# Building a Mamba block's decay arguments by broadcast and a GpSimd clamp instead of small matmuls

## The reference

```
proj = hidden @ in_proj_w.T            # gate | x,B,C | dt
hBC  = silu(conv1d(hBC) )              # 4 taps, causal
dt   = softplus(dt + dt_bias);  A_dt = -exp(A_log) * dt      # 128 heads
A_cumsum = cumsum(A_dt within a chunk of 128 tokens)
Lmat = exp(segment_sum(A_dt))          # exp(cum[l] - cum[s]), l >= s, per head
M = (C @ B.T) * Lmat;  Y_diag = M @ (x * dt)
states = (B * exp(A_cumsum[-1] - A_cumsum)).T @ (x * dt)     # carried over the chunks
Y = Y_diag + (C @ states) * exp(A_cumsum) + D * x
y = rmsnorm(Y) * norm_w * silu(gate);  out = y @ out_proj_w.T
```

## Time and profile before

| | us |
|---|---|
| median of 3 runs | 2141.62 (2141.0 to 2141.75) |
| the profiled execution, its time | 2141.5 |
| its span, first to last instruction | 2139.8 |
| PE busy | 2102.7 |
| DVE busy | 1689.4 |
| ACT busy | 1401.8 |
| POOL busy | 881.4 |
| mean granted TensorE clock | 0.997 |

### The profile page before, as it was taken

How to read it: one execution, slowest core, us unless ns; L and a number is a source line. 1 busy time by engine, 2 the same in 40 slices (tenths; PEclk the granted TensorE clock), 3 DMA queues, 4 the chain that set the end, 5 groups by cost and what they waited for, 6 DMA issues and landing times.

```text
span 2139.8 us, 37480 instructions
## 1 busy us (share of the span) xinstructions
PE 2102.7 (98%) x13386; PEld 1732.0 (81%) x13386; DVE 1689.4 (79%) x2679; ACT 1401.8 (66%) x1918; POOL 881.4 (41%) x622
## 2 busy tenths in 40 slices
PE   7999998999999999999999999999999999999999
PEld 6788876888888888888888888888888888878887
DVE  7555468988888888888898889898888888876554
ACT  5322277878787777777787877787777778752221
POOL 1222134545454545444454544544544545422221
PEclk9999998999999999999999999999999999999999
DMA  5543224233333333232333333342333233255441
GB/s 201 177 146 138 61 94 125 90 109 103 100 112 101 105 96 108 95 122 91 100 112 101 101 98 114 105 122 96 100 101 112 90 104 109 97 186 177 135 147 40
DMA packets 128644, 241.89 MB, mean 113 GB/s; under 512 B 14048, under 2 KB 48608, under 8 KB 128224
## 3 DMA queue, kind: packets, MB, share of 16 engines
q1 hardware_dynamic: 128480, 239.73, 34.9%
HBM read 234.17 MB, written 5.51 MB: 112 GB/s over the span
## 4 chain that ended last, share of the span: by engine, by line
PE 90%; DVE 3%; issue 3%; ACT 2%; DMA 1%; POOL 1%; SPq 0%; DVEq 0%; POOLq 0%; ACTq 0%
PE ring L1013 35%; PE ring L1113 16%; PE bank L412 6%; PE bank_e L412 6%; PE yt L1094 6%; PE st L1078 4%; PE yt L1100 4%; PE xt L1065 3%; PE bank_e L424 3%; PE bank L424 3%; PE arg L1051 2%; PE xt L1026 1%; PE bank L654 1%; DMA w_raw<-w_in 0%; DVE xr L304 0%
## 5 line engine op out<-in xcount | busy, mean ns | idle before, releaser
L1013 PE MATMUL ring<-m_lnt,w_sb 128*128 128x512 f32 x3456 | 859.9, 399 | 1.2 <-DVE xc L1440 1.2
L1013 PEld LDWEIGHTS ring<-m_lnt,w_sb 128*128 128x128 f32 x3456 | 633.0, 189 | 127.1 <-DVE xc L1440 1.5
L1673 POOL TENSOR_TENSOR w_sb<-w_raw,w_sb 128x512 fp32r<-128x512 f32 x288 | 401.7, 1400 | 177.3 <-ACT w_sb L1246 177.0
L1688 POOL TENSOR_TENSOR ysq<-ysq,y 128x512 f32<-128x512 f32 x126 | 162.8, 1292 | 652.8 <-ACT y L1290 652.8
L1113 PE MATMUL ring<-wo,ygs 128*128 128x512 f32 x1536 | 369.4, 390 | 2.0 <-issue 2.0
L1113 PEld LDWEIGHTS ring<-wo,ygs 128*128 128x128 f32 x1536 | 287.3, 188 | 63.2 <-issue 2.6
L1440 DVE SCALAR_TENSOR_TENSOR xc<-ring,cw,xc 128x511 f32<-128x511 f32 (+2 forms) x384 | 286.0, 745 | 23.0 <-ACT xc L1258 13.9
L1258 ACT ACTIVATE xc<-ring,cb,cw 128x512 f32<-128x512 f32 x128 | 99.2, 775 | 215.4 <-PE ring L1013 215.4
L1678 POOL TENSOR_TENSOR wo<-wo_raw,wo 128x512 fp32r<-128x512 f32 x128 | 214.0, 1672 | 0.0
L1246 ACT ACTIVATE w_sb<-w_raw 128x512 fp32r<-128x512 f32 x288 | 177.0, 619 | 26.8 <-DMA w_raw<-w_in 26.8
L1094 PE MATMUL yt<-em,x_dt 128*64 128x128 f32 x2048 | 183.7, 279 | 3.2 <-DVE state L1482 3.2
(11 more groups left out here) (203 smaller groups left out, 3159.2 us busy)
## 6 DMA issues: line engine op xcount, KB each, us to landing
w_raw<-w_in SPq DMA_DIRECT2D x288, 256.0 KB, 4.2
ce<-e_t SPq DMA_DIRECT2D x128, 384.0 KB, 4.1
wo_raw<-w_out SPq DMA_DIRECT2D x128, 256.0 KB, 4.4
f_gu_q<-gu_w SPq DMA_DIRECT2D x28, 512.0 KB, 3.7
f_gu_zr<-gu_z SPq DMA_DIRECT2D x28, 512.0 KB, 4.5
f_gu_sr<-gu_s SPq DMA_DIRECT2D x28, 512.0 KB, 5.3
f_dn_q<-dn_w SPq DMA_DIRECT2D x28, 256.0 KB, 3.5
f_dn_zr<-dn_z SPq DMA_DIRECT2D x28, 256.0 KB, 4.0
```

The lines of the kernel that those rows point to most:

```text
L1013: mm = nc.tensor.matmul(dst[:], w_sb[:, u % WR, wp, k * P:(k + 1) * P], lnt[:, xp, k, b * S:(b + 1) * S], start=(i == 0), stop=(i == 3 * K ...
L1673: nc.gpsimd.tensor_tensor(w_sb[:, u % WR, 1], w_raw[:, u % NR], w_sb[:, u % WR, 0].bitcast(F32), ALU.subtract).then_inc(w_lo, 1)
```

## The change

The argument matmuls go, with all that fed them: the three bfloat16 parts, their stores and four small loads a step, and the memsets of ones. Instead the float32 cumulative sums are stored once (`c_t`) and each step loads the rows of its two heads broadcast over all partitions (`cum_b`, 512 KB). The sums by token stand as a column in `cum_q`, made ahead of the loop by PE. `clamp(k)` on POOL forms min(cum_b - cum_q, 0) in eight instructions of 128x128 (2 heads x 4 chunks). One exp on ACT reads that from SBUF and writes ARG.

Orders change too. ACT takes the exp of step k+1 in step k: in odd steps ahead of the SiLUs, in even steps as the last thing. POOL clamps for k+1 behind w_low of z. DVE does `mask_em(k)` ahead of `scale_x(k)` and `gate(k-1)`. SP loads weights, then wo, then the sums of k+2, then ce. Ahead of the loop the decays come from a matmul with `later` (1 - tri) in place of transposes, the chunk sums from `sum_chunks`, and the projection of ("x", 2) moves behind gram(0) and turn_b(0). `ysq` holds one batch and not two, and `square_sums(0)` moves from step JP + 6 to JP + 1.

```diff
                 def load_args(k):
                     b, h = batch(k), 2 * pair(k)
-                    sp.wait_ge(a_ones, 4)
-                    need(sp, arg_mm, k - 1)
-                    for g in range(2):
-                        at = 32 * g
-                        sp.dma_start(a_right[at:at + 3, k % 2], a_parts[0:3, h + g, b * S:(b + 1) * S])\
-                            .then_inc(a_loaded[k % 2], 16)
-                        sp.dma_start(a_left[at + 3:at + 6, k % 2], a_parts[0:3, h + g, b * S:(b + 1) * S])\
-                            .then_inc(a_loaded[k % 2], 16)
+                    need(sp, exp_done, k - 1)
+                    sp.dma_start(cum_b[:, k % 2], c_t[h:h + 2, b * S:(b + 1) * S]
+                                 .rearrange("(o h) t -> o h t", o=1).to_broadcast([P, 2, S])).then_inc(c_loaded[k % 2], 16)
+
+                def load_decay(k):
...
+                load_units(units_of(-1)[0:6])
+                sp.wait_ge(cum_done, B)
+                sp.dma_start(c_t, cum[:]).then_inc(c_stored, 16)
+                load_units(units_of(-1)[6:])
+                sp.wait_ge(c_stored, 16)
+                load_args(0)
+                sp.wait_ge(cum_exp, 1)
                 sp.dma_start(e_t, e_cum[:]).then_inc(e_stored, 16)
-                sp.wait_ge(parts_stored, 16 * 3)
-                load_args(0)
+                load_units(units_of(1))
+                load_args(1)
+                load_decay(0)
                 for k in range(K):
                     if k > 0:
-                        load_units(k + 1)
-                    if k + 1 < K:
-                        load_args(k + 1)
-                    if k == K - 1:
-
-                        sp.wait_ge(prj_mm, NU)
-                        sp.wait_ge(conv_done, len(CONVED))
-                        tiles.load_gu(sp, 0, 0)
...
-                def arguments(k):
-                    pe.wait_ge(a_loaded[k % 2], 64 * (k // 2 + 1))
-                    need(pe, em_done, k)
-                    if k == 0:
-                        pe.wait_ge(btok_done, 1)
-                        pe.wait_ge(decq_done, B)
-                    for c in range(CPB):
-                        for g in range(2):
-                            rows = slice(32 * g, 32 * g + 6)
-                            mm = nc.tensor.matmul(ARG[:, g, c * CS:(c + 1) * CS],
-                                                  a_left[rows, k % 2, c * CS:(c + 1) * CS],
-                                                  a_right[rows, k % 2, c * CS:(c + 1) * CS], start=True, stop=True)
-                    mm.then_inc(arg_mm, 1)
...
-                def spread_last():
-                    pe.wait_ge(diag_done, B)
-                    pe.wait_ge(adt_done, 2 * B)
-                    nc.tensor.matmul(ST[:], ones[:], pre[:, 0:B * (OFFC - 1) * H], start=True, stop=True)\
-                        .then_inc(last_mm, 1)
-
-                def turn_dec():
-                    pe.wait_ge(rest_done, 4)
-                    pe.wait_ge(adt_done, 2 * B)
+                def cumulate_by_token(b):
+                    pe.wait_ge(adt_done, b + 1)
+                    pe.wait_ge(dtq_done, b + 1)
+                    nc.tensor.matmul((XT, ST)[b][:], tri[:], a_dt[:, b], start=True, stop=True).then_inc(cumq_mm, 1)
+
+                def sum_later(b):
+                    pe.wait_ge(later_done, 1)
+                    pe.wait_ge(adt_done, b + 1)
+                    if b:
+                        pe.wait_ge(cum_done, 1)
+                    nc.tensor.matmul((YT, ARG[:, 0])[b][:, 0:OFFC * H], later[:], a_dt[:, b, 0:OFFC * H],
+                                     start=True, stop=True).then_inc(dec_mm, 1)
+
+                def sum_chunks():
                     pe.wait_ge(cum_done, B)
                     for b in range(B):
-                        for c in range(OFFC):
-                            at = b * S + c * CS
-                            mm = nc.tensor.transpose((XT, ARG[:, 0])[b][:, c * H:(c + 1) * H], dec_h[:, at:at + CS],
-                                                     ident[:])
-                        mm.then_inc(dect_mm, 1)
+                        at = b * (OFFC - 1) * H
+                        mm = nc.tensor.matmul(ARG[:, 1, at:at + (OFFC - 1) * H], ones[:], a_dt[:, b, H:OFFC * H],
+                                              start=True, stop=True)
+                    mm.then_inc(last_mm, 1)
...
                 def exponent(k):
-                    act.wait_ge(arg_mm, k + 1)
-                    part = ARG[:].rearrange("p h t -> p (h t)")
-                    nc.scalar.activation(part, part, ACT.Relu, scale=-1.0).then_inc(arg_clamped, 1)
                     act.wait_ge(arg_clamped, k + 1)
-                    nc.scalar.activation(part, part, ACT.Exp, scale=-1.0).then_inc(exp_done, 1)
+                    need(act, em_done, k)
+                    if k == 0:
+                        act.wait_ge(btok_done, 1)
+                        act.wait_ge(decq_done, B)
+                    nc.scalar.activation(ARG[:], cum_b[:, k % 2], ACT.Exp).then_inc(exp_done, 1)
...
                         tap(("x", k + 1))
                     for unit in ahead[1:2]:
                         w_high(unit)
-                    if k < K:
-                        exponent(k)
                     for g in gram_in(k):
                         copy_btok(g)
                     if k + 1 < K:
+                        if k % 2:
+                            exponent(k + 1)
                         activate_x(k + 1)
                         activate_z(k + 1)
                     if 1 <= k <= K:
@@ -1406,6 +1400,8 @@
                         tap(unit)
...
+                    if k + 1 < K and k % 2 == 0:
+                        exponent(k + 1)
...
                     if 1 <= k < K - 1:
                         conv(("x", k + 1))
-                    if k < K:
-                        scale_x(k)
                     if k == 0:
                         conv(("x", 1))
+                        scale_x(0)
                         decay_c(0)
+                        mask_em(0)
+                    elif k < K:
+                        mask_em(k)
+                        scale_x(k)
                     if 1 <= k <= K:
                         gate(k - 1)
                     if k < K:
-                        mask_em(k)
...
+                def clamp(k):
+                    pool.wait_ge(c_loaded[k % 2], 16 * (k // 2 + 1))
+                    if k == 0:
+                        pool.wait_ge(cumq_done, B)
+                    for h in range(2):
+                        for c in range(CPB):
+                            part = cum_b[:, k % 2, h, c * CS:(c + 1) * CS]
+                            last = nc.gpsimd.tensor_scalar(part, part, cum_q[:, k, c, h:h + 1], 0.0, ALU.subtract, ALU.min)
+                    last.then_inc(arg_clamped, 1)
...
                     for unit in ahead[1:2]:
                         w_low(unit)
+                    if k + 1 < K:
+                        clamp(k + 1)
                     if 1 <= k <= K:
```

More of the change, by code:

```diff
@@ L930, in sync, with load_units @@
             def sync(self, sp, tiles):
-                def load_units(k):
-                    for unit in units_of(k):
+                def load_units(units):
+                    for unit in units:
                         u = UNIT[unit]
@@ L1342, in scalar @@
                 tap(("x", 0))
+                for b in range(B):
+                    act.wait_ge(cum_mm, b + 1)
+                    nc.scalar.activation(cum[:, b * S:(b + 1) * S], ARG[:, b], ACT.Copy).then_inc(cum_done, 1)
                 w_high(("z", 1))
@@ L1366, in scalar @@
+                for b in range(B):
+                    act.wait_ge(dec_mm, b + 1)
+                    part = (YT, ARG[:, 0])[b][:, 0:OFFC * H]
+                    nc.scalar.activation(part, part, ACT.Exp).then_inc(dec_exp, 1)
+                act.wait_ge(last_mm, 1)
+                nc.scalar.activation(e_last[:].rearrange("p b c h -> p (b c h)"), ARG[:, 1], ACT.Exp).then_inc(last_done, 1)
+                w_high(("x", 2))
                 tap(("x", 1))
                 copy_btok(0)
-                act.wait_ge(last_mm, 1)
@@ L1369, in scalar @@
-                nc.scalar.activation(e_last[:].rearrange("p b c h -> p (b c h)"), ST[:], ACT.Copy).then_inc(last_done, 1)
+                exponent(0)
                 def factor_root(b):
```

164 lines of the change are left out of this document (67 added, 97 removed).

## The result

The changed kernel takes 2558.58 us (median of 4 runs, 2555.27 to 2561.68) against 2141.31 (2140.67 to 2141.75, 4 runs): 1.195 times the time before, with a 95% interval of 1.193 to 1.197. It is slower, as forecast, but by 417 us and not by 60. The profiled execution took 2561.68, with a span of 2560.0.

What follows compares the result with a forecast made beforehand. PE was taken as the bound, to be overtaken by a two-step ring. A group: -3.6 + 2.6 + 2.45 + 2.4 = +3.9 us; sixteen groups +62, edges -2: +60 on 2141.5, so 2201.5 us, range 2118 to 2295.

Steps and rivals of the forecast that it cites:

- The ring: Chain of DVE, ACT and POOL work over two plain steps: closes in 24.2 us, where PE needs 22.1.
- VectorE's 9.05: DVE's part of the two-step chain, from y_low to the end of the gate with mask_em ahead: 9.05 us.
- Rival A: Clamps hide and PE stays the bound: 2122 us, or 2085 without the c unit's wait; chance 0.17.
- I take 0.33: Price of one 128x128 clamp piece on POOL: 0.33 us, bounds 0.2 to 0.6; eight are 2.64 a step.
- rival C: GpSimd pays 0.45 to 0.6 us a piece: 2263 to 2345 us, out products also waiting for wo_low; chance 0.18.
- 64 us each: Slope of the clamp's price through four odd exps a group, eight pieces each: 512 us for each us of a piece.
- PE's gain: Argument matmuls gone from PE: 0.45 us a step saved, 3.6 a group of eight, 57 over 127 steps.
- rival E: A projection at half clock follows each group's wait: +2.5 us a group, +40, 2241 us; chance 0.05.
- the b unit: The x projection that reuses the z unit's ring bank waits for SiLU of z: 2.45 us a group.
- the edges of the loop: Work before and behind the loop: -2 us, between -6 and +4.
- rival D: ACT's table loads don't pair up: 1.29 us more every two steps, +83, 2284 us; chance 0.05.
- the c unit: In the step after the c unit the output product waits for wo_low: 2.4 us a group.

Runs made afterwards that it cites:

- e7: Changed kernel with the exp of step k+1 last in ScalarE's step in odd steps too, pieces left in place: 2248.44 us.
- e9: Changed kernel with four of the eight clamp pieces of each step left out: 2253.32 us.
- e2: Changed kernel with the constant 0.5 subtracted in each clamp piece in place of the column of cum_q: 2436.01 us.
- e4: Changed kernel with only the minimum in each clamp piece, the subtraction left out: 2455.49 us.
- e1: Changed kernel with seven of the eight clamp pieces of each step left out: 2170.14 us.
- e8: Changed kernel with GpSimd only subtracting, in two wide instructions a step ahead; ReLU and exp on ScalarE, VectorE's order and ce load reordered as well: 2118.43 us.

## Why the prediction was wrong in size

**Right: the direction and where the cause sits.** The ring through clamp, exp, SiLU and y_high took over from PE, ScalarE waited for the clamp in front of the SiLUs, the busy shares misled. ScalarE's long waits are those of the odd steps (8.14 in the rows above, 2.10 in the even one). e7 shows that it is the exp's place that closes it. But the ring that closed isn't the one drawn: VectorE's 9.05 are not in it, and the even pieces are. Rival A falls with it, since even at the forecast's price the ring (23.36) is longer than what PE needs (22.4). The prediction named pieces far from 0.33 as a sign that it would be wrong, and that is what came.

**Wrong: the price of a piece.** The step that failed is "I take 0.33", with bounds of 0.2 to 0.6. A piece is 0.711, beyond both, and the eight of a step with their waiting for VectorE take 6.27 in the mean (802.1 / 128) where the sum has 2.64. It was drawn from the rows of other instructions as a straight line through two-input instructions of 512 and 256 columns, down to 0.27. The form wasn't on the page. Its own line is 0.29 fixed and 3.28 ns a column, while the copy, with 0.61 for 512 columns, can't have over 1.2 ns for one. The rival C had this cause but stopped at 0.6. Its sign came true: output products wait for wo_low 30 times, twice in nearly every group.

**Wrong: the slope above that price.** 8 x 0.38 = 3.05 us a step more, by 64 us each, would be 195, and by the mean 6.27 it would be 232. From e9 to after it was 305 us for 3.42 us a step (the pieces' totals, 364.1 and 802.1, over 128 steps), 89 for each, close to the 98 to 112 of e2 to e4. From e1 (97.7) to e9 it was 83 us for 2.08, 40 each, where at most one set of pieces in two steps counts. In after the even exp waits too, and both sets are in the ring. "More than linear" was written, but put down to waits of PE in every odd step.

**The rest: 39 us short, with errors that partly cancel.** e9 less the 0.2 us a step that it has above the forecast's price (13 us) is 2240, against 2201.5 and a range of its own that ended at 2235: 39 us for all other terms. PE's gain was 0.30 and not 0.45: +19. Of the 0.36 idle in front of the argument's matmuls nothing came back: the weight loads of the y products now carry that row (L1080, issue, 46.8 us in after, 4.2 in before). The waits in a group came to 5.9 instead of 8.3, the ring being 1.0 shorter than drawn: some -38. The half clock after waits, the rival E, was given 0.05, but it came on top: in e9 PE is busy 2116.4 us against 2070.9 in e8, +45. It should have been a term and not a rival, since the rows for it were there and the b unit's wait was forecast. And the edges of the loop were put at -2, between -6 and +4; the wait at its end is 13.40 in e9: +15. The prediction follows SyncE's new order in the loop and says nothing of its last step. Together +41, for the 39 measured.

**Right: the table loads pair up** (66 and 65 in after for 127 and 127), so the rival D falls. A load costs 1.29 to the start of the next instruction (1187.67 to 1188.96), and starts 0.02 behind the exp's end, so the trace doesn't show the 2.66 that the Trainium skill, "ScalarE: Activation LUTs", section "What ACT_TABLE_LOAD costs", gives for a switch with its drain. Right too is **the c unit**: 2.2 forecast as 2.4. The saved loads bring nothing, as forecast, and their price is the exp in front of the SiLUs. **The b unit**: 3.0 at the forecast's price, 7.6 at the real one.

**The shared port: right on one side, overlooked on the other.** The sum had no price for it, and rightly so for VectorE: the gate's second instruction was not held by the clamps. In after it takes 0.75 in the median beside them, and y_low 0.69 (1.21 before). What was overlooked is that VectorE holds the pieces: eight at 0.711 are 5.69, and they took 6.27.

**DMA**: the clamp stood idle 0.0 us in front of cum_b in after (the row of L1676); nil was right.

## What to carry to other kernels

Before an instruction is moved to another engine, find a row of just this form there; where there is none, double the nearest one for the upper bound, and ask for the price at which the answer changes. Put nothing in front of a chain of short instructions that waits for the slowest engine, even if it saves table loads: the same work last in the step cost 310 us less. When an engine's averages look free, list what each instruction on it waits for, round to itself: that length against the bound's is the forecast. Add up its work for one period, too: GpSimd's 47.93 and 64 pieces of 0.711 are 93.4 us, for a group in which PE needs 96.3. And follow a changed order of loads to the last step.

## What the runs showed of the hardware

A GpSimd instruction with a tensor and a scalar, 128x128 in f32 with two operations, takes 0.711 us: 0.29 fixed (0.07 of it for a column of scalars) and 3.28 ns a column, a line through two widths, 64 and 128 columns; with one operation 0.602. One with two inputs, the second a broadcast column, took 1.91 for 1024 columns, against 2.40 for two full inputs.

Whom GpSimd holds depends on the form. Its two-input instructions can hold a VectorE instruction with two SBUF inputs until a whole gapless run of them is over: 3.85 us (above), and 5.62 for y_low, 0.68 alone, beside four of them in e7. It isn't always so: in before, y_low beside the same splits has a median of 1.21 and at most 1.80.

```profile
786.49 5.62 DVE L1514 TENSOR_TENSOR ygs<-sz,ygs 128x512 fp32r<-128x512 f32 x1
786.54 1.28 POOL L1686 TENSOR_TENSOR ysq<-ysq,y 128x512 f32<-128x512 f32 x1
...
787.79 2.54 POOL L1659 TENSOR_TENSOR w_sb<-w_raw,w_sb 128x512 fp32r<-128x512 f32 x2
...
790.30 1.26 POOL L1664 TENSOR_TENSOR wo<-wo_raw,wo 128x512 fp32r<-128x512 f32 x1
```

The pieces with a scalar hardly held VectorE (0.75 and 0.69 in the median, above), but were slowed by it. In after, the eight from 1168.31 took 6.85 us; the seventh of them took 1.48 while VectorE's product of two SBUF tensors (L1489, 1172.94, 0.95 us) ran. The Trainium skill, "SBUF — State Buffer", section "Who interferes with whom", has the pair as locked for the whole instruction by whoever issues first; the trace shows more on one side (at times a run of instructions) and next to none on the other, and goes before it.

The clock: in after the projection behind a wait of 7.28 us took 5.00 us, at full clock 3.02. In e9, 3.80 idle were followed by 5.49 for it, at a granted clock of 0.50. Waits of some 2.2 us were followed by both levels within one run, as two output products of after show:

```profile
710.34 2.97 PE L1099 MATMUL ring<-wo,ygs 128*128 128x512 f32 x12 [2.18 <-POOL wo L1666]
...
835.20 4.58 PE L1099 MATMUL ring<-wo,ygs 128*128 128x512 f32 x12 [2.17 <-POOL wo L1666]
```

The granted clock was 1.00 over the first and 0.63 over the second. What tells these apart the runs don't show.
